# Attention and ternary feed-forward on one core: feed-forward weights from float32r to bf16, activations to two fp16 pieces, and both batch loops written out

## The reference

```
x = layernorm(x + attention(x))
h = silu((x @ w1.T) * s1) * ((x @ w2.T) * s2)      # 256 -> 1024
h = gelu((h @ h1.T) * s3)                          # 1024 -> 1024
h = gelu((h @ h2.T) * s4)                          # 1024 -> 1024
x = layernorm(x + (h @ w3.T) * s5)                 # 1024 -> 256
```

## Time and profile before

| | before |
| --- | --- |
| median of three runs | 4006.61 us |
| the profiled execution, as timed | 4005.5 us |
| its span, first to last instruction | 4003.7 us |
| mean granted TensorE clock | 0.950 |
| TensorE matmuls busy | 3642.2 us, 91% |
| TensorE weight loads busy | 1954.6 us, 49% |
| VectorE busy | 2552.1 us, 64% |
| ScalarE busy | 2595.1 us, 65% |
| GpSimd busy | 1051.4 us, 26% |
| read and written in memory | 166.63 MB, 108.00 MB |

### The profile page before, as it was taken

One profiled execution on the slowest core, in us unless ns is written; L12 is line 12 of the kernel. 1 busy time (PEld: TensorE's weight loads), 2 busy tenths in 40 slices (PEclk: granted clock), 3 DMA queues, 4 the chain that ended last, 5 costly groups with the idle time before them and its releaser, 6 DMA issues. The chain is left out here.

```text
span 4003.7 us, 70655 instructions
## 1 busy us (share of the span) xinstructions
PE 3642.2 (91%) x20993; PEld 1954.6 (49%) x20993; DVE 2552.1 (64%) x4806; ACT 2595.1 (65%) x3273; POOL 1051.4 (26%) x1024
## 2 busy tenths in 40 slices
PE   5899889989989989989988988869999999999998
PEld 3333333333333323333333332258878787887887
DVE  5778978878878887887897898523333333333333
ACT  2779778868868868877877978734444344443443
POOL 2233434434444343343443342210000000000000
PEclk6989989989989989998998999979999999999999
DMA  4423423422332332333332344210000000000000
GB/s 138 156 70 98 123 77 91 118 81 86 105 95 87 105 107 79 103 95 93 89 117 72 99 123 135 75 51 12 12 12 13 21 11 12 12 11 13 21 11 11
DMA packets 231920, 284.40 MB, mean 71 GB/s; under 512 B 53524, under 2 KB 189908, under 8 KB 230384
## 3 DMA queue, kind: packets, MB, share of 16 engines
q1 hardware_dynamic: 222272, 270.54, 22.5%
q10 hardware_dynamic: 9216, 8.39, 0.6%
HBM read 166.63 MB, written 108.00 MB: 69 GB/s over the span
## 5 line engine op out<-in xcount | busy, mean ns | idle before, releaser
L982 ACT ACTIVATE a_probs<-a_p_s,a_unit_now 128x1024 f32<-128x1024 f32 x1360 | 1448.7, 1111 | 351.9 <-PE a_p_s L1300 345.3
L1086 DVE TENSOR_REDUCE a_part_max<-a_p_r 128x1 f32<-128x512 f32 x2048 | 1301.6, 676 | 270.9 <-PE a_p_r L1313 266.4
L1313 PE MATMUL a_p_r<-a_k_st,a_q_st 48*128 48x512 f16 (+2 forms) x2944 | 921.0, 383 | 209.5 <-DVE a_part_max L1086 126.2
L1313 PEld LDWEIGHTS a_p_r<-a_k_st,a_q_st 48*128 48x128 f16 x2944 | 229.1, 94 | 1239.6 <-DVE a_part_max L1086 871.3
L1642 PE MATMUL p_h<-f_h_hi,f_w_hi 128*128 128x512 f32 x2048 | 807.3, 394 | 24.0 <-issue 24.0
L1642 PE MATMUL p_h<-f_h_lo,f_w_hi 128*128 128x512 f32 x2048 | 803.2, 392 | 0.0
L1330 PE MATMUL a_p_o<-a_probs,a_v_aug 128*17 128x512 f32 (+2 forms) x5888 | 747.5, 588 | 3.5 <-ACT a_raw L992 2.8
L1300 PE MATMUL a_p_s<-a_q_st,a_k_st 50*128 50x512 f16 (+2 forms) x2944 | 694.9, 376 | 25.9 <-ACT a_probs L982 24.0
L1613 DVE TENSOR_TENSOR f_h_lo<-f_h_f,f_h_hi 128x512 fp32r<-128x512 f32 x256 | 177.1, 692 | 697.2 <-ACT f_h_hi L1539 697.2
L1537 ACT ACTIVATE f_h_f<-p_h,f_sc 128x512 f32<-128x512 f32 x256 | 176.6, 690 | 556.7 <-PE p_h L1642 556.6
L1086 DVE TENSOR_REDUCE a_row_max<-a_p_r 128x1 f32<-128x512 f32 (+2 forms) x672 | 427.2, 676 | 98.2 <-PE a_p_r L1313 95.9
(11 more groups left out here) (131 smaller groups left out, 4533.6 us busy)
## 6 DMA issues: line engine op xcount, KB each, us to landing
qk_scratch<-a_qk_room SPq DMA_DIRECT2D x288, 128.0 KB
a_w_lo<-wqkv_inner SPq DMA_DIRECT2D x30, 768.0 KB, 4.3
a_q_st<-qk_scratch SPq DMA_DIRECT2D x64, 192.0 KB, 3.7
a_k_st<-qk_scratch SPq DMA_DIRECT2D x64, 192.0 KB, 4.8
a_a_lo<-a_attn SPq DMA_DIRECT2D x384, 32.0 KB, 2.0
a_o_lo<-wo_inner SPq DMA_DIRECT2D x24, 512.0 KB, 3.7
a_qk_room<-wf SPq DMA_DIRECT2D x22, 512.0 KB, 3.8
w_lo_scratch<-a_qk_room SPq DMA_DIRECT2D x22, 512.0 KB, 2.7
```

What stands on the lines that cost most here:

```text
L982: act.activation(probs[:, s % 2, 2 * p:2 * p + 2, :], p_s[:, 2 * p:2 * p + 2, :], ACT.Exp, scale=unit_now[:, lvl:lvl + 1]).then_inc(exp_do ...
L1086: dve.reduce_max(out, src, AX.X).then_inc(max_read.sem, 1)
L1313: ins = pe.matmul(p_a[:, r * size:(r + 1) * size], q_st[rows_of(j, ROWS), query_at:query_at + 128], k_st[rows_of(j, ROWS), key_at:key_at + ...
```

## The change

**Feed-forward numbers.** The weights of w1, w2, h1 and h2 are kept as bf16 (`w_hi`, 20 chunks) and w3 as float32r (`w3`). A chunk's rest is cut twice more, to a middle and a low bf16 part, which are used only if the flag is set. Activations become two fp16 pieces (`xt_hi`, `xt_lo`, `h_hi`, `h_lo`), the last ones, which `narrow` reads, two float32r pieces (`last_hi`, `last_lo`). So that fp16 can hold them, x is multiplied by 2^11 when it is cut, and h by powers of two. Those come from a bound on the values that is computed once at the start of `ffn` from the largest absolute values of the weights and scales.

```diff
-                        act.activation(xt_hi[:, c, :], p_t[:, c, :], ACT.Copy).then_inc(t_hi.sem, 1)
+                        act.activation(xt_hi[:, c, :], p_t[:, c, :], ACT.Copy, scale=X_UNIT).then_inc(t_hi.sem, 1)
...
-                        act.activation(h_hi[:, (half + v // 8) % 2, v % 8, :], h_f[:, v % 2, :], ACT.Copy).then_inc(deep_hi.sem, 1)
+                        if v < 16:
+                            act.activation(h_hi[:, 1, v % 8, :], h_f[:, v % 2, :], ACT.Copy, scale=up[:, 1:2]).then_inc(deep_hi.sem, 1)
+                        else:
+                            act.activation(last_hi[:, v % 8, :], h_f[:, v % 2, :], ACT.Copy).then_inc(deep_hi.sem, 1)
...
-                        dve.tensor_tensor(out=xt_lo[:, c, :], in0=p_t[:, c, :], in1=xt_hi[:, c, :], op=ALU.subtract)\
+                        dve.scalar_tensor_tensor(out=xt_lo[:, c, :], in0=p_t[:, c, :], scalar=X_UNIT, in1=xt_hi[:, c, :], op0=ALU.mult, op1=ALU.subtract)\
...
-                    terms = [(stationary[0], moving[0]), (stationary[1], moving[0]), (stationary[0], moving[1])]
-                    terms = [t for t in terms if t[0] is not None and t[1] is not None]
+                    terms = [(stationary[0], moving[0]), (stationary[0], moving[1])]
+                    terms += [(a, c) for n, a in enumerate(stationary[1:]) for c in moving[:2 - n]]
...
-        xt_hi, xt_lo = sb("xt_hi", [128, 2, 512], F32R), sb("xt_lo", [128, 2, 512], F32R)
-        h_hi, h_lo = sb("h_hi", [128, 2, 8, 512], F32R), sb("h_lo", [128, 2, 8, 512], F32R)
+        xt_hi, xt_lo = sb("xt_hi", [128, 2, 512], F16), sb("xt_lo", [128, 2, 512], F16)
+        h_hi, h_lo = sb("h_hi", [128, 2, 8, 512], F16), sb("h_lo", [128, 2, 8, 512], F16)
+        last_hi, last_lo = sb("last_hi", [128, 8, 512], F32R), sb("last_lo", [128, 8, 512], F32R)
```

```diff
-            with engine.Fori(0, N - 1) as i:
-                steps(in_order(body, later), lambda k: (i, k), plan_body)
+            for i in range(N - 1):
+                steps(in_order(body, later), lambda k, i=i: i + k, plan_body)
...
-            for half in range(2):
-                step(0, half, half)
-            with engine.Fori(0, B - 2) as b:
-                for half in range(2):
-                    step((b, 1), half, (b * 2, 2 + half))
-            for half in range(2):
-                step(B - 1, half, 2 * B - 2 + half)
+            for hh in range(2 * B):
+                step(hh // 2, hh % 2, hh)
```

```diff
-    steps_of_chunk = (("fload", 0), ("fhi", 1.9), ("flo", 2.3), ("fstore", 3.4))
...
+    for n in range(PER_BATCH):
+        at = STEPS + CHUNK_AT + CHUNK_GAP * n
+        body += [(at + by, kind, 1, n) for kind, by in (("fload", 0), ("fhi", 1.9), ("fout", 2.8), ("flo", 2.3), ("flow", 4.8), ("fstore", 6.4))]
+        body += [(at + 4.6 + .5 * part, "fcheck", 1, 2 * n + part) for part in range(2)]
+    body.append((STEPS + CHUNK_AT + CHUNK_GAP * PER_BATCH - .4, "ffold", 1, 0))
+    for n in range(W3_CHUNKS):
+        at, m = W3_AT + W3_GAP * n, PER_BATCH + n
+        end += [(at + by, kind, 0, m) for kind, by in (("fload", 0), ("fhi", 1.9), ("flo", 2.3))]
+        end += [(at + 3.2 + .5 * part, "fcheck", 0, 2 * m + part) for part in range(2)]
+    end.append((W3_AT + W3_GAP * W3_CHUNKS, "ffold", 0, 1))
+    end += [(TOP_AT + TOP_GAP * n, "ftop", 0, n) for n in range(TOPS)]
     end += [(piece.at, "fplace", 0, n) for n, piece in enumerate(PLACES)]
...
-                            pool.tensor_tensor(out=f_raw.bitcast(F32R), in0=f_raw, in1=f_cut, op=ALU.subtract).then_inc(f_lo_done.sem, 1)
+                            if n >= PER_BATCH:
+                                part = slice((n - PER_BATCH) * HCOLS, (n - PER_BATCH + 1) * HCOLS)
+                                pool.tensor_tensor(out=f_w3_lo[:, part], in0=f_raw, in1=f_w3[:, part], op=ALU.subtract).then_inc(f_lo_done.sem, 1)
+                                continue
+                            pool.tensor_tensor(out=f_cut[:, 1, :], in0=f_raw, in1=f_cut[:, 0, :], op=ALU.subtract).then_inc(f_mid_done.sem, 1)
+                            pool.wait_ge(f_mid_done.sem, f_mid_done.value(it, n + 1))
+                            pool.sem_inc(held.sem, 1)
+                            pool.tensor_tensor(out=f_raw, in0=f_raw, in1=f_cut[:, 0, :], op=ALU.subtract).then_inc(f_lo_done.sem, 1)
+                        elif kind == "flow":
+                            pool.wait_ge(f_lo_done.sem, f_lo_done.value(it, n + 1))
+                            pool.sem_inc(held.sem, 1)
+                            f_hi_out.wait(pool, it, n + 1)
+                            pool.sem_inc(held.sem, 1)
+                            pool.tensor_tensor(out=f_cut[:, 0, :], in0=f_raw, in1=f_cut[:, 1, :], op=ALU.subtract).then_inc(f_low_done.sem, 1)
```

## The result

The changed kernel takes 3862.2 us (median of 4 runs, 3858.4 to 3865.0) where the kernel before takes 4009.4 beside it: a ratio of 0.963, 95% interval 0.961 to 0.965. The profiled spans are 4003.7 and 3857.9 us, a difference of 145.8.

A forecast was written before the change was run, and what follows sets the result against it. TensorE (91% busy) sets feed-forward's pace; in attention TensorE, VectorE and ScalarE are close. Sum: -55.3 - 36.5 - 12 - 7.5 - 1 + 2 + 4 + 1.5 = -104.8 from 4005.5, plus 1.1: 3902 us; range 3864 to 3958.

The forecast's parts named there:

- Feed-forward pace: Feed-forward's 5120 matmuls turned 16-bit go from 226.8 to 216 ns each, saving 55 us.
- rival D: In the 5120 feed-forward matmuls, mixed bf16 and fp16 is not a single pass: 5060 us at two passes; chance 0.03.
- A: Rival: feed-forward's 16-bit matmuls go no faster than float32r, limited by something both formats share: 3957 us; chance 0.09.
- Feed-forward loop: Writing out the feed-forward loop removes five jumps back of 7.3 us each, saving 36.5 us.
- remaining `If`s: One branch per feed-forward half batch stays, taken to fit under queued matmuls; otherwise 15 would give back 13 us.
- Start of feed-forward: First x load leaves 0.9 us sooner, and the new chain of bounds runs under it: gain 1 us.
- Attention loop: Attention loop written out: x load 3.9 us earlier, less 1.9, net 2 us an edge, 12 us for six.
- rival B: Attention edges come back whole because GpSimd's added work fits its gaps: 46 instead of 12 us, 3868; chance 0.11.
- The 1.9 us: At each attention edge, new work delays SP's packing queue: 1.3 us from GpSimd plus 0.6 from SP.
- TensorE's wait for x: At an attention edge TensorE arrives earlier at the same wait, which grows longer than 7.3 us.
- The removed register arithmetic buys nothing: Attention's register arithmetic before waits runs on sequencers ahead of full engines, so removing it gains nothing.
- End of attention: Earlier, halved weight placements free GpSimd's last fetch, gaining 7.5 us; maxima cost 4 us, another W3 chunk 1.5.

The follow-up runs named there:

- ffn_out: The kernel before with only the feed-forward loop written out: 3976.3 us, ratio 0.993.
- pe_loop: The changed kernel with the attention loop put back on TensorE's queue alone: 3894.3 us, ratio 0.972.
- small_parts2: The changed kernel with GpSimd's added subtractions working on one column of 1024 in 20 of the 21 chunks: 3859.9 us, ratio 0.964.
- att_out: The kernel before with only the attention loop written out: 3966.4 us, ratio 0.989.

## Why the prediction was right and wrong

**Feed-forward pace: right.** 215.9 ns against the 216 taken. 5120 x (226.8 - 215.9) would be 55.8 us; 16 half batches gained 16 x (81.57 - 78.36) = 51.4. The difference is the mix: `narrow` rose from 227 to 232 ns (512 x 5.7 = 2.9 us), and the eight 16-bit matmuls between two groups of it take 1.74 us, 217.5 ns. Of bf16 weights against fp16 activations the rows show a single pass at that pace, so rival D is out, and A with it. The Trainium skill's N / 2.4 GHz plus 2.5 ns (TensorE: Matmul & The Clock Gate, Part 1) agrees with this row, 215.7 against 215.9, and not with float32r, 226.8. The Trainium skill's statement that both 16-bit formats are widened to one inner format (FP8 and Floating Point Precision, "TensorE Precision Notes") is in keeping with the single pass; the format itself no run here shows.
**Feed-forward loop: right.** The five stretches with a jump lost 6.5 to 7.4 us each, 35.6 in all, against 36.5; ffn_out shows it alone. The remaining `If`s opened one gap, of 1.6 us, where the text had none. From the first `wide` matmul to the end the part gained 85.6 us where these two terms had 91.8.
**Start of feed-forward: wrong in size, small.** The x load left 1.7 us sooner behind the last attention matmul, but nothing came of it: from that matmul to the first `wide` one it was 30.1 us and is 29.9. TensorE of the changed kernel there:

```profile
2582.59 1.97 PE L1683 MATMUL p_t<-ident_sb,f_xa 128*128 128x128 f32 x8 [1.86 <-DMA f_xa<-x]
2587.36 0.61 PE L1673 MATMUL p_h<-f_xt_hi,f_w_hi 128*128 128x512 f16 x1 [2.80 <-issue]
```

Here nothing is queued over the `If` in front of `wide` and it is bare, 1.4 us of it on the chain. TensorE's branch there takes 4.70 us (from 2582.6), and 0.37 in the kernel before; it takes 4.4 to 4.8 in seven of the changed kernel's variants but 0.38 in pe_loop. What decides this is open.
**Attention loop: the step that failed.** The text took 3.9 us for the x load and took 1.9 away for GpSimd and SP; 2 us an edge. Steps 24 to 30 gained 6.5 us at each of the six edges, 39 us in all, near the 7.7 that stood as its upper bound (rival B had 7.7 x 6 = 46 and was given 0.11; its reason, that GpSimd's added work fits its gaps, is what small_parts2 shows). Three things were wrong in it. The 1.9 us do not exist: the 16 packing issues start 4.0 us ahead of step 24 where they started 3.9 ahead (only the four issues before them come 1 us later), they take 2.1 us less in the mean, 2.7 at the first edge, since TensorE does not jump beside them, and small_parts2 shows the rest hidden. The x load won 4.6 us in the mean, not 3.9. And TensorE's own jump, which was given nothing, did count, by way of those issues: 1.9 us an edge in pe_loop. Together x is loaded 7.0 us earlier in the batch, and the edge is 6.5 shorter. TensorE's wait for x, which was to grow beyond 7.3 us, was between 7.1 and 8.0 us at the six edges and is between 4.1 and 4.7:

```profile
525.41 0.60 PE L1314 MATMUL a_p_r<-a_k_st,a_q_st 48*128 48x512 f16 x1 [4.67 <-DVE a_part_max L1081]
```

From one x load to the next the batch period fell from 317.2 to 307.8 us, 9.4 us where the text said 2 and called more than 5 a sign that it is wrong.
**"The removed register arithmetic buys nothing": wrong.** att_out gained 9 us in steps 40 to 84, where no jump is: 1.0 to 1.2 us in each of the seven batches inside the loop, in pieces of 0.07 to 0.17 at some eleven steps, and 1.2 at one step of the last batch. Step 76 of batch 3, 3.85 us in the changed kernel, takes 3.93 with ScalarE alone in a loop, 80 ns between two activations with a register operation between them. In steps 40 to 84 ScalarE's loop alone took back 3 us, TensorE's 3 and SP's 1; the other 2 are not placed. An engine ahead of which work is queued is not the same as an engine that never waits for its sequencer.
**A part of the change without a term.** The move of `fcheck` by 1.4 steps is in the diff, and I passed over it. It is worth 6 us alone and 20 with the loop written out. Together, by the traces: 43 + 20 less 3 for the rest is 60; the recorded terms of attention (12 + 7.5 - 2 - 4 - 1.5) made 12.
**End of attention: wrong by 6 us.** GpSimd's last sum, against the earlier trace rows:

```profile
2561.45 1.26 POOL L887 TENSOR_TENSOR a_c_f<-a_d_room 128x512 f32<-128x512 f32 x1 [9.15 <-DMA a_fine_room<-up_far]
```

It still waits 9.15 us instead of 10.42, with no placement beside the fetch. So the placements had cost it some 1.3 us, not 7.5. The rest belongs to the fetch itself; which part of it (its late issue or its small transfers) was not tried. In the last batch the twelve maxima, which start in step 56, cost 2.7 us in steps 56 to 69 (4 forecast), and the second W3 chunk, which ScalarE and GpSimd cut in step 33, 1.45 us in steps 33 to 36 (1.5 forecast).
**The sum.** Attention gained 60.0 us by the trace where 12 were forecast, feed-forward 85.6 for 91.8, between them 0.2 for 1: 145.8 for 104.8. The range reached down to 3864, less than one measured edge below its own rival B, since only "part of B" had been taken in; two unpriced gains of the same sign (9 us of register arithmetic, 20 of `fcheck`) went past it. That it was missed by only 1.8 us is luck: feed-forward and the end of attention were each forecast 6 us too good and hid part of the error.

## What to carry over

Before pricing a jump, look what each engine issues right behind it: here SP's branch alone made one transfer late and cost 33 us, TensorE's alone slowed SP's issues ahead of the same transfer and cost 32 with what it did elsewhere, and all five engines' together cost 42 to 54, less than the two added up. An instruction that nobody needs soon still holds a full in-order engine if its input is late, so each moved line of a hand-written order deserves a term, also where it looks like bookkeeping. Bring a load forward only behind the last reader of its buffer: six steps gained 11 us, nine steps lost 12.

## What was not expected of the hardware

- A float32r matmul of 512 columns takes 226.8 ns among its like and 232 ns in groups of four between 16-bit ones; 16-bit ones take 215.9 and 217.5.
- Around TensorE's jump back in its loop, three of 16 DMA issues on SP take 1.0 to 2.0 us instead of 0.59 (one of the 72 counted took 0.83); without TensorE's jump at most one does.
- A wait behind register arithmetic made the time between two of ScalarE's activation starts 0.865 us instead of 0.786, though nothing else that the profile shows held it; between most other pairs of the same steps it cost nothing.
- The branch of a half batch's `If` takes 3.3 to 3.9 us on TensorE also in a program without loops. Under queued matmuls 14 of 16 cost nothing in the changed kernel. The one in front of the first `wide` takes 4.70 us there and 0.37 in the kernel before.
- 118 semaphore clears in a row take SP 6.9 us, each some 59 ns.
